# Turned maxima in the projections' ring of banks, and one output projection three places later

## The reference

```python
xn = _adaln(x, noise_emb, ln1_w, ln1_b)
q, k, v = split(xn @ qkv_w.T);  q = _rope(q);  k = _rope(k)
x = res + _attn(q, k, v) @ sa_out_w.T              # self-attention
xn = _adaln(x, noise_emb, ln2_w, ln2_b)
q = _rope(xn @ q_w.T);  k = _rope(context @ k_w.T);  v = context @ v_w.T
x = res + _attn(q, k, v) @ ca_out_w.T              # cross-attention
xn = _adaln(x, noise_emb, ln3_w, ln3_b)
x = res + gelu(xn @ ffn_w1.T + ffn_b1) @ ffn_w2.T + ffn_b2
```

## The kernel before

| user | read out by | semaphore |
| --- | --- | --- |
| scores | ACT, the sum of exponentials (L769) | total_done |
| weigh | ACT, the exponential (L783) | exp_done |
| max_turn | ACT, max_copy (L751) | rows_placed |
| mix | DVE, o_low (L903) | o_lo_done |
| product of k or q | DVE, the rotation's second product (L859) | rope_taken |
| product of v | DVE, the copy (L866) | v_done |
| product of o | DVE, the addition to the residual (L872) | res_added |
| turn_x | DVE, scale and shift (L923) | x_full |
| mod | ACT, mod_copy (L705) | mod_copied |

## Time and profile before

### The profile page before, as it was taken

How to read it: one execution, slowest core, us unless ns; L and a number is a source line. 1 busy time by engine, 2 the same in 40 slices (tenths; PEclk the granted TensorE clock), 3 DMA queues, 4 the chain that set the end, 5 groups by cost and what they waited for, 6 DMA issues and landing times. The chain is left out here.

```text
span 1903.4 us, 38411 instructions
## 1 busy us (share of the span) xinstructions
PE 1867.2 (98%) x13460; PEld 1631.8 (86%) x13460; DVE 1285.6 (68%) x2241; ACT 1429.7 (75%) x3811; POOL 801.9 (42%) x834
## 2 busy tenths in 40 slices
PE   8899999999999999999999999999999999999999
PEld 7788888888878888988988987688898988989898
DVE  5877666767777776776776776346766667666754
ACT  5788878888888898888888899655656566666654
POOL 3534333433443454454454444104535445353531
PEclk9999999999999999999999999999999999999999
DMA  7777777676687687677677688433131322323131
GB/s 219 206 210 209 216 207 204 188 206 188 186 232 212 196 236 221 192 222 220 190 217 223 193 226 201 130 111 122 56 111 56 112 78 93 97 73 105 46 99 34
DMA packets 307375, 311.46 MB, mean 164 GB/s; under 512 B 22000, under 2 KB 259952, under 8 KB 307184
## 3 DMA queue, kind: packets, MB, share of 16 engines
q1 hardware_dynamic: 306576, 308.67, 56.0%
q10 hardware_dynamic: 608, 0.34, 0.1%
HBM read 212.46 MB, written 92.27 MB: 160 GB/s over the span
## 5 line engine op out<-in xcount | busy, mean ns | idle before, releaser
L769 ACT ACTIVATE ps_s<-ps_s,neg_max 128x256 f32<-128x256 f32 x1024 | 461.6, 454 | 52.0 <-DVE neg_max L884 48.8
L884 DVE TENSOR_REDUCE neg_max<-ps_s 128x2 f32<-128x512 f32 x512 | 349.1, 686 | 202.7 <-PE ps_s L640 202.0
L783 ACT ACTIVATE prob<-ps_s 128x512 f32<-128x512 f32 x512 | 307.8, 602 | 89.2 <-PE ps_s L661 85.0
L965 POOL TENSOR_TENSOR rope_c<-rope_c,rope_s 128x256 f32<-128x256 f32 x128 | 98.5, 769 | 316.1 <-DVE rope_s L859 316.1
L640 PE MATMUL ps_s<-kT,qT 96*128 96x256 f32 x1024 | 218.1, 294 | 9.2 <-ACT ps_s L769 4.9
L769 ACT ACTIVATION_READ_ACCUMULATOR ps_s<-ps_s,neg_max 128x1 f32 x1024 | 217.7, 213 | 0.0
L640 PEld LDWEIGHTS ps_s<-kT,qT 96*128 96x128 f32 x1024 | 168.4, 190 | 56.9 <-ACT ps_s L769 21.9
L661 PE MATMUL ps_s<-qT,kT 112*128 112x256 f32 x1024 | 207.7, 285 | 9.6 <-ACT ps_s L769 8.8
L630 PE MATMUL ps_g<-xx_hi,w_hi 128*128 128x256 f32 x1024 | 208.7, 285 | 1.8 <-issue 1.4
L630 PE MATMUL ps_g<-xx_hi,w_lo 128*128 128x256 f32 x1024 | 206.1, 283 | 0.0
L630 PE MATMUL ps_g<-xx_lo,w_hi 128*128 128x256 f32 x1024 | 205.7, 282 | 0.0
(11 more groups left out here) (157 smaller groups left out, 4714.3 us busy)
## 6 DMA issues: line engine op xcount, KB each, us to landing
kT<-k_turned SPq DMA_DIRECT2D x384, 128.0 KB, 3.3
qT<-q_turned SPq DMA_DIRECT2D x128, 256.0 KB, 4.0
f_raw<-in_w1T SPq DMA_DIRECT2D x124, 256.0 KB, 3.0
k_turned<-rot_hi SPq DMA_DIRECT2D x64, 256.0 KB, 3.2
k_turned<-rot_lo SPq DMA_DIRECT2D x64, 256.0 KB, 2.5
q_turned<-rot_hi SPq DMA_DIRECT2D x64, 256.0 KB, 3.8
q_turned<-rot_lo SPq DMA_DIRECT2D x64, 256.0 KB, 4.2
qT<-q_turned SPq DMA_DIRECT2D x128, 128.0 KB, 4.1
```

The source lines that it names most:

```text
L769: ins = eng.activation(scores[:, t * L:(t + 1) * L], scores[:, t * L:(t + 1) * L], ACT.Exp, bias=neg_max[G % 2][:, t, j:j + 1], accum_out= ...
L783: eng.activation(prob[:, n % NP, :, :].rearrange("p t l -> p (t l)"), ps_s[:, score_bank(step), :], ACT.Exp).then_inc(exp_done, 1)
L884: eng.tensor_reduce(neg_max[G % 2][:, :, j], ps_s[:, score_bank(step), :].rearrange("p (t l) -> p t l", l=L), AX.X, ALU.max, negate=True). ...
L965: eng.tensor_tensor(rope_c[n % 2][:, 0, :], rope_c[n % 2][:, 0, :], rope_s[:, 0, :], ALU.subtract)
```

## The change

`max_turn` leaves the list of the scores' ring and enters that of the projections' ring. Its transposes go to `ps_g`, `max_copy` reads `ps_g`, and `bank_left` gets its semaphore, `rows_placed`. The sizes of the rings stay (five and three banks). In the table, the output projection fed in during item N - 3 = 29 (that of item 28) begins at p + 58 instead of p + 55. No instruction is added or taken away.

```diff
-            spread(p + {B - 2: 61, N - 1: 51}.get(i, 55), 14 if i >= N - 2 else ...
+            spread(p + {B - 2: 61, N - 3: 58, N - 1: 51}.get(i, 55), 14 if i >= N - 2 else ...
...
-        elif (step[0] == "project" and step[4] == 0) or step[0] in ("mod", "mod_turn", "early"):
+        elif (step[0] == "project" and step[4] == 0) or step[0] in ("mod", "mod_turn", "early", "max_turn"):
...
-    score_users = [step for step in order if step[0] in ("scores", "weigh", "max_turn", "mix")]
+    score_users = [step for step in order if step[0] in ("scores", "weigh", "mix")]
...
+                if old[0] == "max_turn":
+                    return rows_placed, nth[old]
...
-                return {"scores": total_done, "weigh": exp_done, "max_turn": rows_placed, "mix": o_lo_done}[old[0]], nth[old]
+                return {"scores": total_done, "weigh": exp_done, "mix": o_lo_done}[old[0]], nth[old]
...
-                            ins = eng.transpose(ps_s[0:MROWS, score_bank(step), t * P:(t + 1) * P],
+                            ins = eng.transpose(ps_g[0:MROWS, bank(step), t * P:(t + 1) * P],
...
-                                       ps_s[ROWS:MROWS, score_bank(("max_turn", G)), 0:L].unsqueeze(1).broadcast_to([2 * HG, OH, L]),
+                                       ps_g[ROWS:MROWS, bank(("max_turn", G)), 0:L].unsqueeze(1).broadcast_to([2 * HG, OH, L]),
```

More of the change, by code:

```diff
@@ L132, in stage_order @@
             put(p + 37, "res_load", i - 1)
-            spread(p + {B - 2: 61, N - 1: 51}.get(i, 55), 14 if i >= N - 2 else 10 if i in (B - 2, B - 1) else 9, [("project", "o", i - 1, t, c) for cs in (range(KC - 1), (KC - 1,)) for t in range(T) for c in cs])
+            spread(p + {B - 2: 61, N - 3: 58, N - 1: 51}.get(i, 55), 14 if i >= N - 2 else 10 if i in (B - 2, B - 1) else 9, [("project", "o", i - 1, t, c) for cs in (range(KC - 1), (KC - 1,)) for t in range(T) for c in cs])
             put(p + (72 if i == B - 2 else 66), "store", i - 1)
```

## The result

| | before | after |
| --- | --- | --- |
| median of six runs each | 1906.32 us | 1914.99 us |
| lowest and highest | 1905.27, 1909.34 | 1913.1, 1918.48 |
| profiled execution, device time | 1905.51 | 1915.65 |
| its span | 1903.4 | 1913.6 |

The ratio is 1.0045, with a 95% interval of 1.0032 to 1.0058: 8.7 us slower, with 6.1 to 11.1 us inside the interval. Lines of the changed kernel are two further on than before: L642 is `scores`, L649 `max_turn`, L663 `weigh`, L632 the projections of q and k, L771 the sum of exponentials.

The account below looks back on a forecast made before the run. PE was taken as the bound, so only its waits could be won. 5.6 + 2.7 + 0.9 - 1.3 = +7.9 us on the median 1908.3 gave 1916.2; forecast range 1913.5 to 1918.5, chance 0.70.

Parts of the forecast that it names:

- The signs: PE waits: five at k for DVE, twelve at weighings replacing the scores' stops; items about 0.1 shorter, items 4 to 7 1.3 longer.
- The stops: Twelve scores stops of 0.42 us behind second max_turns go; the next weighing leaves 0.11 each, 1.3 us won.
- The second product of k, items 4 to 7: Second product of k waits for DVE to read the first from the same bank: 4 x 1.4 = 5.6 us lost.
- The same in item 14: Second product of k of item 16, computed in item 14, waits for DVE's reading of the first: 2.7 us lost.
- The pair at the end of item 13: Two stops, 1.03 and 0.53 us, go, but the weighing at 568.20 waits as much longer for ACT: nothing won.
- The output projection: In item 29 ring waits make mix 58 some 1.3 us late; 0.9 us lost, bounds 0 and 1.4.
- The first max_turn: At 62.21 it waits some 1.4 us for a rotation, hidden by ACT's wait for DMA-brought weights: nothing lost.
- the tail: Stops at the end of the cross-attention, ACT busy nearly throughout: nothing counted, at most 1 us won.
- the stops come back whole: Rival: ACT's chain follows PE, so 7.6 us are won against 9.2 lost, giving 1910; chance 0.17.
- the k waits are hidden: Rival: all 8.3 us at k in items 4 to 7 and 14 hidden, stops back whole, giving 1902; chance 0.05.
- rival 3: Slower: tighter ring at the turned input, or the first max_turn's 1.4, adds 3 to 5 us, giving 1920; chance 0.08.

Follow-up runs that it names:

- e4: Kernel before, with odd groups' max_turns except 59 in the projections' ring and ACT's rotation split of q's second product one place later in self-attention: 1900.74 us, ratio 0.9974.
- e3: Kernel before, with only each item's second max_turn (odd groups, without 59) in the projections' ring, no projection moved: 1905.01 us, ratio 0.9997.
- e2: Kernel before, with only the max_turns of groups 8, 10, 12, 14 and 28 in the projections' ring: 1913.36 us, ratio 1.0039.
- e6: Kernel before, with only the output projection of item 28 three places later, all max_turns in the scores' ring: 1907.46 us, ratio 1.0005.
- e8: Kernel before, with only ACT's rotation split of q's second product one place later in the self-attention: 1906.25 us, ratio 0.9998.
- e7: Kernel before, with only the max_turn of group 0 in the projections' ring: 1906.82 us, ratio 1.0001.
- e1: Changed kernel, but max_turns of groups 8, 10, 12, 14 and 28 stay in the scores' ring: 1907.14 us, ratio 1.0005 against the kernel before.
- e5: Kernel before, with only group 59's max_turn in the projections' ring and the output projection of item 28 three places later: 1907.49 us, ratio 1.0004.

## Why the prediction was right

It said 1916.2 with the forecast between 1913.5 and 1918.5; the median was 1915.0. The signs that it named came: four waits of 1.15 us and one of 2.44 at the second products of k, twelve weighings that wait in place of the twelve scores, an even item shorter by 0.09 and items 4 to 7 longer by 1.30 net, and no change in the cross-attention's even flow. Term by term:

- **The stops, -1.3.** Right in mechanism and size: 0.09 us an item instead of 0.11, so about -1.1. That the rest of the 0.42 is held back by ACT's queue at the next weighing was argued from the earlier trace rows; e4 shows it, by taking one instruction of 0.6 us out of that queue and getting 0.48 an item. The Trainium skill (Perfetto Trace Analysis, Optimization Strategy) reads a repeating gap as possible lack of room in SBUF or PSUM. That agrees with the cause of the stop, and e3 shows how little of it the room returned: 0.09 of 0.42 us.
- **The second product of k, items 4 to 7, +5.6.** Right: 1.40 each, and e2 has the same 1.40 without any other part of the change.
- **The same in item 14, +2.7.** Right: 2.68. With the four before it, this is rule and row together. The Trainium skill (Perfetto Trace Analysis, Matmuls) wants matmul groups to rotate through banks so that reading one overlaps the next. Three banks do that here only while the third user back is not the step's own neighbour; where it is, the trace of the changed kernel has 1.4 and 2.7 us; e2 has the same 1.4, and in item 14 its product begins the same 2.60 us late.
- **The pair at the end of item 13, 0.** Right: the difference goes from +6.06 at head 226 to +4.40 at head 228 and is back at +6.04 at head 230. The 1.03 and 0.53 us of the two stops went into two weighings. One waits 0.55 where it didn't wait before, and the one that waited 1.54 waits 2.51:

```profile
569.59 0.51 PE L663 MATMUL ps_s<-qT,kT 112*128 112x256 f32 x2 [0.55 <-ACT ps_s L771]
574.24 0.50 PE L663 MATMUL ps_s<-qT,kT 112*128 112x256 f32 x2 [2.51 <-ACT ps_s L771]
```

- **The output projection, +0.9.** The size came out: mix 58 is 1.37 later, where I worked out 1.3, and 0.80 is left by head 495. The reason is only half right. The ring's waits stand where they were put, but e6 loses about 1.3 us without them, by the place alone. And what is left is known to about half a microsecond: e8, whose order in this part is that of the kernel before, also gains 0.57 from head 486 to head 495, and e7 loses 0.09.
- **The first max_turn, 0.** Right, and by the cover that was named: e7 shows the wait, no loss behind it, and ACT's wait for the DMA shorter by 0.9 to 1.2 us. The +1.51 that stands at head 24 in the profiled executions is not of group 0. It is a stretch at half clock behind the weighing of head 8 (first row below), where the changed kernel takes 4.36 us to the scores of head 22 and the kernel before 2.74: 1.62 us. The second row below takes 0.97 us where the same four transposes take 0.60 elsewhere. In e3, which leaves group 0 where it was, the same stretch takes 4.31; in e1, which moves group 0 and has the same wait of 1.64 us, it takes 2.74. So it goes with the execution.

```profile
87.96 0.51 PE L663 MATMUL ps_s<-qT,kT 112*128 112x256 f32 x2 [1.64 <-ACT ps_s L771]
88.30 0.97 PE L600 MATMUL ps_g<-ident,xn 128*128 128x128 f32 x4
```

**What the sum left out.** At heads 243 and 244 I counted nothing, and 1.07 us came back. Two things stand there in the kernel before. The scores of head 243 stop for ACT behind max_turn 29, and ACT itself waits for a DMA that carries away a rotated half of k; the row of before, and the same step in the changed kernel:

```profile
602.17 0.63 ACT L745 ACTIVATE rot_hi<-rope_c 128x512 fp32r<-128x512 f32 x1 [0.74 <-DMA k_turned<-rot_lo]
```

```profile
609.72 0.63 ACT L747 ACTIVATE rot_hi<-rope_c 128x512 fp32r<-128x512 f32 x1
```

Neither alone gives the 1.07. Where only the stop is gone, the next weighing takes it back as far as ACT waits for the DMA: e3 has 0.89 us of that wait and keeps 0.09, e4 has 0.75 and keeps 0.19, e1 has 0.52 and keeps 0.50. Where k of item 16 is late and the stop stays (e2), ACT has no such wait and 0.53 comes back. The changed kernel has neither and gets 1.07. The length of this DMA wait also differs between executions that change nothing near it (0.73 us in e5, 0.39 in e6, none in e7, where 0.24 comes back), so a part of the 1.07 may be chance.

In the tail, which I had let off with nothing or a gain of 1 us at most, 1.59 us were lost between heads 495 and 511. PE there, in the changed kernel and in the kernel before:

```profile
1201.04 0.74 PE L663 MATMUL ps_s<-qT,kT 112*128 112x256 f32 x2 [1.83 <-ACT ps_s L771]
1201.71 3.31 PE L678 MATMUL ps_s<-prob,v_kept 128*32 128x256 f32 x32
```

```profile
1192.59 0.50 PE L661 MATMUL ps_s<-qT,kT 112*128 112x256 f32 x2 [1.03 <-ACT ps_s L769]
1193.02 1.93 PE L676 MATMUL ps_s<-prob,v_kept 128*32 128x256 f32 x32
```

The wait before the weighing is 1.83 instead of 1.03 us, but only because PE comes to it earlier: the weighing begins 8.45 us later than in the kernel before, and the scores ahead of it at head 505 were 8.46 later. The loss is in the 32 matmuls behind it, 3.31 instead of 1.93: the clock was at its lower level, as the window says (columns as above):

```profile
1200.00:1205.00 5.00, 3.96 (x35) 1.89 (x35) 0.00 (x0) 3.78 (x15) 0.00 (x0) 0.66 0.39 120
```

Nor is this the change's doing. e8, whose order in this part is that of the kernel before, loses 1.57 us at the same place, behind the same 1.03 us of wait as the kernel before, and e7 loses 1.65; e1, which has the changed kernel's order there and its wait of 1.83, loses 0.04. The rows of e8, then that of e1:

```profile
1191.23 0.80 PE L662 MATMUL ps_s<-qT,kT 112*128 112x256 f32 x2 [1.03 <-ACT ps_s L770]
1191.96 3.19 PE L677 MATMUL ps_s<-prob,v_kept 128*32 128x256 f32 x32
```

```profile
1194.43 0.50 PE L669 MATMUL ps_s<-qT,kT 112*128 112x256 f32 x2 [1.83 <-ACT ps_s L777]
```

So the profiled execution of the changed kernel has, behind its start, two stretches at the lower clock (at 88 and 1201 us) and that of the kernel before one (behind the weighing at 78.27). The one more costs some 1.6 us, which is why the profiled execution, at +10.14, stands above both the sum of 7.9 and the medians' 8.7. Between 7.9 and 8.7 the medians can't decide.

**The number itself.** The three runs that it was made against had a median 2.0 us above that of the six, while the sum was 0.8 short of the measured difference. The two errors have opposite signs and leave 1.2 us. With the median of the six the same sum would have given 1914.2, closer and still in the range; so the base was no help, and being right did not rest on it.

**The rivals.** That the stops come back whole fell with the new waits at the weighings, and e4 shows on what it would have depended. That the k waits are hidden fell with e2: DVE and ACT run dry behind them. The tighter turned input of rival 3 cost nothing that the trace shows: no wait for `xT`'s or the turned input's reading stands in the even flow.

## What to carry to other kernels

Before giving a stopped step a new bank, find what the next step behind it waits for: a stop of 0.42 us was worth 0.09 while the same ACT queue held the following weighing, and 0.48 once one instruction had left that queue. Where a user joins a small ring, walk through every place where three unrelated users meet; 59 of the 64 max_turns joined at a cost that the interval of e1 can't tell from nothing, and the five others cost 7.4 us by e2's median (8.3 at their own places in the trace of the changed kernel) and set the sign. A step may stay in its old ring in just those places, as in e1, e3 and e4: nothing in this kernel asks for all calls of one step to be in one ring.

## What the runs showed of the hardware

The granted clock of PE fell from 2.4 to 1.2 GHz for a short stretch behind single waits in a flow that was busy otherwise, and the length of the wait alone doesn't decide it. Behind the same wait at the same place it fell in one execution and not in another: 1.03 us (fell in e7 and e8, not in the kernel before at 1192.59), 1.64 us at head 8 (fell in the changed kernel, not in e1), 1.83 us in the tail (fell in the changed kernel, not in e1), 2.51 and 2.52 us in item 14 (fell in e1, not in the changed kernel), and 2.44 us at k of item 16, where it didn't fall in the changed kernel and in e2 the row behind the wait took 0.80 instead of 0.50 us, so it did:

```profile
590.34 0.80 PE L638 MATMUL ps_g<-xx_hi,w_hi 128*128 128x256 f32 x2 [2.44 <-DVE rope_s L867]
```

Behind the 1.15 us at the second product of k in items 4 to 7 it never fell, in the changed kernel or in e2. Each fall cost 1.1 to 1.65 us (1.62 and 1.59 in the changed kernel, 1.60 in e1, 1.65 in e7, 1.57 in e8, 1.3 in e2, 1.1 in e4). Differences of that size between two single executions of this kernel are therefore no evidence on an edit; the medians and the length of an item in the even flow are.
